# A graph network's convolutions on one core: one load of four places, addresses ahead of the last wait, fewer waits on wiped slices

## The chip, the cores and the metric

The kernel runs on 1 core of one Trainium2 chip. A core has TensorE (PE; its weight loads are listed as PEld), VectorE (DVE), ScalarE (ACT), GpSimd (POOL) and SyncE (SP), each with an instruction queue of its own, run by a sequencer. They meet only at semaphores. The metric is the device time of one execution in microseconds.

## The reference, cut to what matters

```python
# layer 0: layer norm, relu, an edge network, gather * message, segment sum, added to x
# layer 1: layer norm, relu, and then
def _rgcn_conv(x, src, dst, etype, basis, comp, root, bias):
    n = x.shape[0]                                    # 12500
    r = comp.shape[0]                                 # 8 relations
    W = jnp.einsum('rb,bio->rio', comp, basis)
    seg = dst * r + etype                             # 212500 edges
    agg = jax.ops.segment_sum(x[src], seg, num_segments=n * r)
    cnt = jax.ops.segment_sum(jnp.ones_like(seg, x.dtype), seg, num_segments=n * r)
    mean = (agg / jnp.maximum(cnt, 1.0)[:, None]).reshape(n, r, -1)
    return jnp.einsum('nri,rio->no', mean, W) + x @ root + bias
h = _rgcn_conv(x, src, dst, edge_type, basis1, comp1, root1, bias1)
h = jax.nn.relu(h)
out = _rgcn_conv(h, src, dst, edge_type, basis2, comp2, root2, bias2)
```

All features are 128 wide, all in float32. The two calls of `_rgcn_conv` are the two passes that the change touches; before them stand the sorting of the edges and layer 0.

## The kernel before, in words

`convolve` is called twice, with `which` = 0 and 1. The edges lie sorted by target. They are cut into 1661 columns of 128 edges (`NCOL`), four columns to a group (`TG`; the last group has one), 416 groups (`NG`). The 12500 nodes are 98 blocks of 128 (`NBLK`); a block's edges fill about 17 columns (`PERIOD`).

For each column, in every pass:

- GpSimd gathers the 128 source rows from DRAM into a slot of `got` (L2126). `got` holds 8 groups (`NGA`). GpSimd may gather group g when all columns up to group g - 8 have been through TensorE (`need(pool, s_pass, ...)`), so it runs up to 32 columns ahead.
- VectorE writes a one-hot matrix of the column's targets, `compare` (L2216), eight columns ahead, into `share` or `hot`.
- TensorE multiplies both into a PSUM bank of the column (L2138, two matmul instructions). In pass 0 it also counts the edges (L2141). Four banks are used in turn, so TensorE waits for the sum of the column four before (`s_sum`). It raises `s_pass`.
- VectorE adds the bank, 16 targets by 8 relations wide, to a ring of sums that holds six blocks (`RING`), at a place that was computed earlier and lies in SBUF: `add_column`. It reads the place into a register (`value_load`, L2231), forms the address (L2235, a register instruction), and adds (L2235, SCALAR_TENSOR_TENSOR). In pass 0 the counts are added with the sums, so this add is 128x256 instead of 128x128.

When a block's columns are complete (`closing_at(group)`), there is block work: TensorE spreads the inverse counts (L2165, two matmuls of 512 columns in each half), VectorE multiplies the block's slice of the ring by them (`weigh`, L2250, in two halves), ScalarE wipes the slice (L2191), TensorE multiplies by the eight relation matrices (L2157) and the root matrix (L2153), and SyncE stores the result and fetches rows of the next blocks.

What sets the order is each engine's program alone: it is written out by hand, unrolled, with no scheduler. `need` issues a wait if the value is above zero. Waits are gathered until the next instruction; where it has more of them than one instruction can carry, they become semaphore instructions of their own, recorded at L104.

An add must wait for three things beside its own bank: the preceding add (`s_sum`, since both can touch the same places), the wipe of the slice that the ring comes round to (`s_wiped`), and the join of the ring's 16 extra columns past its end to its beginning (`s_tail`, raised twice at each join).

## Time and profile before

| | us |
|---|---|
| median of 3 runs | 8354.52 (8352.68 to 8361.07) |
| span of the profiled execution | 8476.2 |
| TensorE busy (share) | 6081.7 (72%) |
| GpSimd busy | 5225.1 (62%) |
| VectorE busy | 4272.2 (50%) |
| ScalarE busy | 1968.7 (23%) |
| mean granted TensorE clock | 0.704 |

The profiled execution is one of its own, and the page gives its span, from first to last instruction; it is 121.7 us above the median of the timed runs. Shares are taken over the whole span, which has stages with different limits. The convolutions begin with the first gather of L2126. "Idle before" in a row is the time in which the engine did nothing just before these instructions, and the arrow names what ended it; "issue" there means that the profile shows nothing that the engine waited for. An engine's name with a q (DVEq) is its sequencer: such instructions aren't counted as busy.

### The profile page before, as it was taken

How to read it: one execution, taken by the hardware profiler on the slowest of the kernel's cores; microseconds unless marked ns; L12 is line 12 of the kernel's file. 1: busy time of each engine (PE TensorE's matmuls, PEld its weight loads, DVE VectorE, ACT ScalarE, POOL GpSimd, SP SyncE). 2: the span in 40 equal slices, each digit the busy share in tenths (PEclk: the TensorE clock that was granted, in tenths of full speed). 3: DMA queues.
4: the chain of work that ended last, by engine and by line, in shares of the span. 5: the costliest groups of instructions: out<-in, count | busy, mean ns of one | idle time of the engine just before them, and what ended most of it. 6: DMA issues, size and time to landing. Idle time of an engine off the chain costs nothing. (4 is left out here: it accounts for less than half of the span.)

```text
span 8476.2 us, 125307 instructions
## 1 busy us (share of the span) xinstructions
PE 6081.7 (72%) x31388; PEld 4489.2 (53%) x31388; DVE 4272.2 (50%) x13389; ACT 1968.7 (23%) x3891; POOL 5225.1 (62%) x5105
## 2 busy tenths in 40 slices
PE   5777777778888876777777877665666666666666
PEld 4555555556777765555555555443444444444444
DVE  6544454547888864554555555553333333333333
ACT  4444444445444433111111111110000000000000
POOL 3555555557888876666666666664665665665664
PEclk8877777779999987556556566666565565565666
DMA  5444444448999974111111111111111111111111
GB/s 148 128 131 124 130 125 126 118 111 180 190 192 191 188 162 146 50 51 49 50 50 50 50 49 51 50 50 37 48 48 47 48 49 47 47 48 47 47 48 38
DMA packets 816681, 750.03 MB, mean 88 GB/s; under 512 B 126421, under 2 KB 719249, under 8 KB 815637
## 3 DMA queue, kind: packets, MB, share of 16 engines
q1 hardware_dynamic: 578020, 401.11, 17.7%
q0 software_dynamic: 237296, 340.25, 17.6%
q8 instruction: 276, 4.52, 0.2%
q14 instruction: 459, 3.76, 0.1%
q10 hardware_dynamic: 630, 0.39, 0.0%
HBM read 574.58 MB, written 165.86 MB: 87 GB/s over the span
## 5 line engine op out<-in xcount | busy, mean ns | idle before, releaser
L2126 POOL DMA_INDIRECT got<-h_dram,etcol x3322 | 3147.7, 948 | 1993.1 <-issue 954.2
L2235 DVE SCALAR_TENSOR_TENSOR hacc<-bank,hacc 128x256 f32 (+1 forms) x3322 | 1185.0, 357 | 2839.8 <-issue 1463.1
L2138 PE MATMUL bank<-share,got 128*128 128x128 f32 x4436 | 1275.4, 410 | 773.4 <-DVE hacc L2235 535.9
L2138 PEld LDWEIGHTS bank<-share,got 128*128 128x128 f32 x4436 | 968.2, 278 | 1352.0 <-issue 1290.7
L1611 POOL DMA_INDIRECT msg_dram<-total,idx x1008 | 971.6, 964 | 869.9 <-DVE total L1362 596.6
L1626 POOL DMA_INDIRECT acc_dram<-total,idx x653 | 1023.5, 1567 | 214.3 <-issue 206.1
L2165 PE MATMUL bank<-rcnt,chosen 7*128 7x512 f32 (+45 forms) x784 | 738.5, 1040 | 461.8 <-DVE umade L2250 236.1
L2191 ACT ACTIVATE hacc<-ones_f 128x2048 f32<-128x2048 f32 (+1 forms) x196 | 290.8, 1483 | 2659.8 <-DVE umade L2250 1883.5
L2138 PE MATMUL bank<-hot,got 128*128 128x128 f32 x2208 | 633.8, 408 | 372.6 <-DVE hacc L2235 240.1
L2138 PEld LDWEIGHTS bank<-hot,got 128*128 128x128 f32 x2208 | 479.1, 275 | 657.0 <-issue 632.5
L2157 PE MATMUL bank<-wrel,umade 128*128 128x128 f32 x3136 | 684.2, 406 | 28.2 <-DVE umade L2250 25.0
L2157 PEld LDWEIGHTS bank<-wrel,umade 128*128 128x128 f32 x3136 | 633.5, 309 | 71.4 <-DVE umade L2250 46.8
L2216 DVE TENSOR_SCALAR share<-iota_f,dstcol 128x128 f32<-128x128 f32 x2218 | 659.2, 298 | 15.7 <-PEq L1970 10.6
L1358 DVE SCALAR_TENSOR_TENSOR soft<-bank,neg_b,log1p 128x512 f32<-128x512 f32 x416 | 311.5, 749 | 637.4 <-ACT log1p L1234 357.3
L1112 PEld LDWEIGHTS bank<-w,soft 128*128 128x128 f32 x3328 | 547.2, 233 | 74.4 <-issue 50.4
L1103 PE MATMUL bank<-edges_t,w 128*128 128x512 f32 x830 | 524.8, 714 | 50.8 <-issue 46.7
L1112 PE MATMUL bank<-w,soft 128*128 128x128 f32 x3328 | 542.7, 317 | 0.0
L2165 PEld LDWEIGHTS bank<-rcnt,chosen 7*128 7x128 f32 (+45 forms) x784 | 183.4, 290 | 559.0 <-issue 558.0
L1095 PE MATMUL bank<-ident,edges 128*128 128x128 f32 x1656 | 324.4, 307 | 154.1 <-issue 141.4
L2187 ACT ACTIVATE flat<-bank 128x128 f32<-128x128 f32 x196 | 54.4, 278 | 1610.7 <-issue 929.1
L1212 ACT ACTIVATE edges_t<-bank 128x512 f32<-128x512 f32 x414 | 248.0, 599 | 776.3 <-remote 682.6
L1128 PE MATMUL bank<-win,to_edge 128*128 128x128 bf16 x4992 | 396.9, 236 | 31.1 <-DVE total L1362 19.9
(263 smaller groups left out, 8275.8 us busy)
## 6 DMA issues: line engine op xcount, KB each, us to landing
edges<-in_edge_attr SPq DMA_DIRECT2D x415, 256.0 KB
unit<-msg_dram SPq DMA_DIRECT2D x616, 129.0 KB
got<-h_dram,etcol POOLq DMA_INDIRECT x3322
low<-rows_dram SPq DMA_DIRECT2D x164, 256.0 KB
win<-split_dram SPq DMA_DIRECT2D x416, 96.0 KB
low<-rows_dram SPq DMA_DIRECT2D x252, 128.0 KB
acc_dram<-zeros SPq DMA_DIRECT2D x200, 128.0 KB
made<-acc_dram SPq DMA_DIRECT2D x147, 128.0 KB, 3.2
```

What stands on the lines that cost most here:

```text
L1095: ins = nc.tensor.transpose(bank_t[:, j * P:(j + 1) * P], edges[s.slot(NE, 0)][:, j, :], g.ident[:, :])
L1103: nc.tensor.matmul(bank_z[s.slot(2, 1) if two_banks else 0][:, :], g.w1[:, :], edges_t[s.slot(2, 1)][:, :], start=True, stop=True).then_in ...
L1112: ins = nc.tensor.matmul(bank_e[:, j * F:(j + 1) * F], soft[k][:, j * P:(j + 1) * P], g.w2[:, :], start=False, stop=True, skip_group_check ...
L1128: ins = nc.tensor.matmul(bank[:, j * F:(j + 1) * F], to_edge[k][:, j, :], win[s.slot(NE, 2)][:, part * F:(part + 1) * F], start=windows.ow ...
L1611: pool.indirect_dma_start(g.msg_dram[:, :], bass.IndirectOffsetOnAxis(ap=idx[k][:, j:j + 1], axis=0), total[k][:, j, :], None).then_inc(s_ ...
L1626: pool.indirect_dma_start(g.acc_dram[j][:, :], bass.IndirectOffsetOnAxis(ap=idx[k][:, j:j + 1], axis=0), total[k][:, j, 0:F], None, comput ...
L2126: pool.indirect_dma_start(got[k][:, j, :], None, g.h_dram[which][:, :], bass.IndirectOffsetOnAxis(ap=source[:, c:c + 1], axis=0)).then_inc ...
L2138: ins = nc.tensor.matmul(columns[j][:, 0:P], got[k][:, j, :], equal, start=True, stop=True)
L2157: ins = nc.tensor.matmul(to, weighted[t % 2][:, r * P:(r + 1) * P], g.wrel[which][:, r * F:(r + 1) * F], start=False, stop=r == R - 1)
L2165: nc.tensor.matmul(bank_s, chosen[t % 2][0:t + 1, :], rates_all[0:t + 1, half * HALF:(half + 1) * HALF], start=True, stop=True).then_inc(s ...
L2216: v.tensor_scalar(hot[group % NHOT][:, j, :], g.iota_f[:, :], g.dstcol[:, c:c + 1], None, ALU.is_equal).then_inc(s_node, 1)
L2235: v.scalar_tensor_tensor(to, columns[j].rearrange("p (a n) -> p a n", n=NARROW), 1.0, to, ALU.mult, ALU.add).then_inc(s_sum, 1)
```

## The change

The places of a group are read by one load of four registers, without the assertion on their range. The address is formed ahead of the wait for TensorE's pass, which is now asked for last. The waits for the wiped slice and for the tail are issued only in groups where the number waited for has grown since the group before.

```diff
-            def add_column(c):
+            def load_places(group):
+                first = group * TG
+                _, at = nc.values_load_multi_w_load_instructions(
+                    place[:, first:first + g.columns(group)], engines=[mybir.EngineType.DVE], min_val=0, max_val=RING * P - 1,
+                    skip_runtime_bounds_check_because="a column's lowest target less the multiple of the ring's rows below it")
+                return at
+
+            def laps(group):
+                return len(range(RING, g.closed(group), RING))
+
+            def add_column(c, at):
                 group, j = divmod(c, TG)
-                if j == 0:
+                if j == 0 and (group == 0 or g.closed(group - 4) > g.closed(group - 5)):
                     need(dve, s_wiped, done_before + g.closed(group - 4))
-                    need(dve, s_tail, laps_before + 2 * len(range(RING, g.closed(group), RING)))
-                at = dve.value_load(place[:, c:c + 1], min_val=0, max_val=RING * P - 1)
+                if j == 0 and (group == 0 or laps(group) > laps(group - 1)):
+                    need(dve, s_tail, laps_before + 2 * laps(group))
                 to = ring[:, 0:SUMMED, bass.ds(at, NARROW)]
+                need(dve, s_sum, c)
+                dve.lower_ap(to)
                 dve.wait_ge(s_pass, c + 1)
-                need(dve, s_sum, c)
                 v.scalar_tensor_tensor(to, columns[j].rearrange("p (a n) -> p a n", n=NARROW), 1.0, to, ALU.mult, ALU.add).then_inc(s_sum, 1)
...
+                at = load_places(group) if group < NG else ()
                 for j in range(TG):
                     c = group * TG + j
                     if c < NCOL:
-                        add_column(c)
+                        add_column(c, at[j])
```

On VectorE, at the beginning of a group of the first pass in which a block is weighed, the order before is this. TENSOR_LOAD reads a place, "ISA x2" are a register instruction and the assert, "ISA" forms the address; `c_pass_0` and `c_sum_0` are `s_pass` and `s_sum`, `c_counts_0` is `s_wiped`, `u_left_0` is `s_tail`, `u_mm_0` and `c_low_0` are what TensorE raises in the block work.

```order
L2231 TENSOR_LOAD srccol [waits u_left_0,c_counts_0]
L2231 ISA x2
L2235 ISA [waits c_sum_0,c_pass_0]
L2235 SCALAR_TENSOR_TENSOR hacc<-bank,hacc 128x16x16
L2216 TENSOR_SCALAR hot_0<-iota_f,dstcol 128x128 [waits c_pass_0]
L2250 TENSOR_TENSOR umade_0<-bank,hacc 128x512 [waits u_left_0,u_mm_0,c_sum_0,c_low_0]
L2231 TENSOR_LOAD srccol
L2231 ISA x2
L2235 ISA [waits c_sum_0,c_pass_0]
L2235 SCALAR_TENSOR_TENSOR hacc<-bank,hacc 128x16x16
L2216 TENSOR_SCALAR hot_0<-iota_f,dstcol 128x128 [waits c_pass_0]
```

The same two columns of the same group after the change, on VectorE:

```order
L2229 TENSOR_LOAD srccol
L2246 ISA [waits c_sum_0]
L2248 SCALAR_TENSOR_TENSOR hacc<-bank,hacc 128x16x16 [waits c_pass_0]
L2216 TENSOR_SCALAR hot_0<-iota_f,dstcol 128x128 [waits c_pass_0]
L2263 TENSOR_TENSOR umade_0<-bank,hacc 128x512 [waits u_left_0,u_mm_0,c_sum_0,c_low_0]
L2246 ISA [waits c_sum_0]
L2248 SCALAR_TENSOR_TENSOR hacc<-bank,hacc 128x16x16 [waits c_pass_0]
L2216 TENSOR_SCALAR hot_0<-iota_f,dstcol 128x128 [waits c_pass_0]
```

The load stands once for the group, register instruction and assert are gone, and of the two waits on the address one has moved to the add. In this group neither the wiped slice nor the tail is waited for by the add. Over a pass, VectorE issues 415 loads, 1661 address instructions (96 with one more wait, 8 with two more) and the same adds, compares and block work. The other engines' programs are as before.

## Rows read from the trace of the kernel before

**Rows 1.** The page: the span, and GpSimd's gathers (busy, mean | idle before).

```profile
span 8476.2 us, 125307 instructions
L2126 POOL DMA_INDIRECT got<-h_dram,etcol x3322 | 3147.7, 948 | 1993.1 <-issue 954.2
```

**Rows 2.** Busy time by engine in two windows, first and second pass.

```profile
3289.00:5810.00 2521.00, 1863.06 (x7384) 1308.69 (x7384) 1260.96 (x3738) 265.93 (x388) 1574.46 (x1661) 0.61 0.19 49
5810.00:8457.00 2647.00, 1678.24 (x5774) 1178.81 (x5774) 981.66 (x3650) 161.64 (x296) 1573.26 (x1661) 0.60 0.18 47
```

**Rows 3.** Timeline of GpSimd (start, length): a run of 12 gathers, the next start.

```profile
5985.84 0.95 POOL L2126 DMA_INDIRECT got<-h_dram,etcol  x1 [1.63 <-PE bank L2138]
...
5999.59 0.95 POOL L2126 DMA_INDIRECT got<-h_dram,etcol  x1 [0.30 <-issue]
6004.59 0.95 POOL L2126 DMA_INDIRECT got<-h_dram,etcol  x1 [4.05 <-PE bank L2138]
```

**Rows 4.** Timeline of GpSimd: ends of the passes, and a short pause.

```profile
3289.03 1.04 POOL L2126 DMA_INDIRECT got<-h_dram,etcol  x1 [3.54 <-issue]
...
5774.23 0.95 POOL L2126 DMA_INDIRECT got<-h_dram,etcol  x1 [0.30 <-issue]
5835.05 0.98 POOL L2126 DMA_INDIRECT got<-h_dram,etcol  x1 [59.87 <-issue]
...
5888.91 0.94 POOL L2126 DMA_INDIRECT got<-h_dram,etcol  x1 [0.30 <-issue]
5891.35 0.94 POOL L2126 DMA_INDIRECT got<-h_dram,etcol  x1 [1.50 <-issue]
...
8425.34 0.95 POOL L2126 DMA_INDIRECT got<-h_dram,etcol  x1 [4.26 <-PE bank L2138]
```

**Rows 5.** The chain of waits (start, length, what), two adds in ordinary flow.

```profile
8409.53 0.29 DVE hacc L2235
...
8410.38 0.29 DVE hacc L2235
```

**Rows 6.** Busy time by engine (PE, PEld, DVE, ACT, POOL) around the run of rows 3.

```profile
5985.80:5992.20 6.40, 5.17 (x16) 2.85 (x17) 3.63 (x16) 0.28 (x1) 4.84 (x6) 0.72 0.23 62
5992.20:6002.80 10.60, 4.91 (x13) 2.58 (x12) 2.28 (x7) 0.00 (x0) 6.51 (x7) 0.50 0.19 50
6002.80:6010.60 7.80, 6.53 (x30) 5.92 (x30) 3.27 (x13) 1.35 (x2) 3.79 (x4) 0.60 0.13 34
```

**Rows 7.** The chain of waits late in a run of gathers.

```profile
8416.30 0.69 DVEq L2231
...
8419.84 0.70 DVEq L2235
```

**Rows 8.** Timeline of VectorE late in a run of 44 gathers, adds only.

```profile
5875.88 0.29 DVE L2235 SCALAR_TENSOR_TENSOR hacc<-bank,hacc 128x128 f32 x1 [6.51 <-issue]
...
5882.88 0.29 DVE L2235 SCALAR_TENSOR_TENSOR hacc<-bank,hacc 128x128 f32 x1 [6.51 <-issue]
...
5889.88 0.29 DVE L2235 SCALAR_TENSOR_TENSOR hacc<-bank,hacc 128x128 f32 x1 [6.51 <-issue]
...
5898.29 0.29 DVE L2235 SCALAR_TENSOR_TENSOR hacc<-bank,hacc 128x128 f32 x1 [7.92 <-issue]
```

**Rows 9.** Sequencer instructions, 5868 to 5890 us (ns min/median/max).

```profile
L2231 DVEq TENSOR_LOAD <-srccol x3: 690/707/707, 5873.0 to 5887.0; - x3
...
L2235 DVEq FUSED_REGOPS  x3: 701/710/710, 5871.6 to 5885.6; - x3
...
L104 DVEq EVENT_SEMAPHORE  x3: 702/702/702, 5870.2 to 5884.2; - x3
```

**Rows 10.** Sequencer instructions of line L2231 over the whole run.

```profile
L2231 DVEq TENSOR_LOAD <-srccol x3322: 1/301/1409, 3288.7 to 8455.9; - x196
...
L2231 DVEq SEQ_ASSERT  x3322: 1/23/1039, 3289.2 to 8456.5; - x196
```

**Rows 11.** All gathers, line L2126, by duration (ns min/median/max).

```profile
L2126 POOL DMA_INDIRECT got<-h_dram,etcol x3322: 942/947/1045, 3289.0 to 8425.3; - x196
```

## What I predict

> **What bounds the kernel now.** I read the page first, for where the time lies. The two convolutions run from 3289.0 us to the end at 8476.2, 5187 of 8476 us; no engine is busy over 75% of either [rows 1, 2]. They are what the change touches. GpSimd issues one gather per column, 3322 in all. Each call is busy 0.95 us and is followed by 0.30 us of its own; in an unbroken run the calls start 1.25 us apart [rows 3]. 1661 columns by 1.25 us are 2076 us. The first pass spends 2486 us from its first gather to the end of its last (3289.03 to 5775.2), the second 2591 us (5835.05 to 8426.3); between and behind stand tails of 59.9 and 49.9 us [rows 1, 4]. 2486 + 60 + 2591 + 50 = 5187. So GpSimd stands still for some 410 and 515 us, waiting for columns to be consumed (the ring `got` holds 8 groups of 4 columns). TensorE is busy 1863 and 1678 us [rows 2], by 98 blocks 19.0 and 17.1 us a block of 17 columns, where GpSimd needs 21.2 us. TensorE could keep up; VectorE's turn is what is late.
>
> Next the chain of waits, for VectorE's own pace. In ordinary flow one column takes 8410.38 - 8409.53 = 0.85 us [rows 5], and it is the sequencer's: load, register arithmetic, assert, semaphore, address (load and assert in [rows 10]), with the add of 0.29 us and the compare lying over them. 0.85 is under 1.25, so this pace alone doesn't hold GpSimd back. What does is seen in the second half of each long run of gathers. Take the run of [rows 6]: GpSimd starts a run of 12 calls at 5985.84 and ends it at 6000.54 [rows 3]. In its first 6.4 us VectorE starts 16 instructions; in the next 10.6 us only 7; then, with the run over, 13 in 7.8 us. The chain there shows why: each sequencer step of VectorE takes 0.70 us or a multiple of it, where an assert took 0.02 us and a load 0.30 [rows 7, 10]. In the long first run of the second pass (44 gathers without a pause) it settles at exactly 7.00 us a column [rows 8]. A column has five sequencer instructions there, each recorded at about 0.70 us [rows 9]. Where a group begins there is a sixth (a separate semaphore wait), and the distance is 8.41 us. So each sequencer instruction costs 1.40 us, two steps of 0.70, while the vector work itself costs nothing extra. It comes only while GpSimd has been issuing for a while, and ends about 2 us after it pauses. I call it stepping. It is what leaves VectorE behind, and it makes the number of *sequencer* instructions the quantity to count.
>
> **The change, part by part.** Counts are those of the emitted order.
>
> 1. One load for four places, no assert. Before, each column has a load, a register instruction and an assert; after, there is a load for each group: 3 x 1661 = 4983 become 415 a pass.
> 2. The address is computed ahead of the last wait. Before, two waits stand ahead of the add: one becomes a separate semaphore instruction, the other sits on the address. After, `s_sum` sits on the address and `s_pass` on the add itself, so 1661 separate instructions go. The handover from TensorE to the add no longer has the address computation in it; I give it no time, since GpSimd's pitch covers it.
> 3. Waits on a wiped slice and the tail only where the count has grown: of some 405 separate instructions a pass 104 remain (96 columns with one extra wait, 8 with two).
>
> The 192 products of a pass keep their two separate waits, 380 or so. Sequencer instructions a pass: 415 + 1661 + 104 + 380 = 2560, against 5 x 1661 + 405 + 380 = 9090. By column 1.54 against 5.47; in steps of 0.70 us 3.08 against 10.9. Vector work is the same. Nothing is moved on another engine.
>
> In ordinary flow the column falls from 0.85 us to about the two vector instructions (starts 0.2 to 0.35 us apart, with the wait for the preceding sum): I take 0.5 to 0.6. By itself that gains nothing, since GpSimd's 1.25 covers it; with stepping gone it would leave GpSimd as the bound. While stepping, a column falls from 7.6 us (10.9 x 0.70) to 3.08 x 0.70 = 2.16 us, which is still over 1.25.
>
> How much of the time is stepped? I treat it as a store that fills. Before: 6.4 us of ordinary flow are 7.5 columns, 82 steps, while 6.4 / 0.70 = 9 drain; so it holds about 72. After: TensorE allows (17 / 19.0 + 17 / 17.1) / 2 = 0.94 columns a us, so 2.90 steps a us come in and 1.43 drain; the store is full after 72 / 1.47 = 49 us instead of 6.4. In that time the consumers gain (0.94 - 0.80) x 49 = 6.9 columns on GpSimd. Then, stepping, the consumers take 1 / 2.16 = 0.46 a us, GpSimd catches up in 6.9 / 0.34 = 20 us and must pause. A stepped group takes 8.6 us and its gathers 5.0, so the pause is 3.6 us, and ends the state. A cycle of 49 + 20 + 4 = 73 us has 69.5 us of gathers: 1.25 x 73 / 69.5 = 1.317 us a column, 2188 us a pass. The tails empty the ring; at 0.6 instead of 0.85 us for up to 32 columns they lose 8 to 10 us each: 50 and 40.
>
> Sum: 3289 + 2 x 2188 + 90 = 7755 us, 721 below the profiled 8476.2. The timed median, 8354.5, lies 122 us below the profiled span already. I carry the difference over: 8354.5 - 721 = 7633 us.
>
> The load of four registers isn't in the trace. The nearest row is the load of one, 0.30 us [rows 10]. Its bounds are 0.30 and four times that, 1.2 us a group. Either lies under cover: a group needs 2 to 2.4 us of VectorE in ordinary flow and 5.0 of GpSimd. If while stepping it cost as four loads (eight steps), that would be 6 more steps a group, 4.58 a column. The same cycle is then 25 + 7 + 4 us, 1.39 us a column, 240 us more in all: 7875. I take two steps, as its row shows for one load.
>
> A rule that speaks against the change: a gather takes 942 to 1045 ns over both passes [rows 11], although VectorE runs one compare of 128x128 f32 for each. In the 6.4 us with 16 vector instructions its calls are as short as elsewhere [rows 3, 6]. So nothing is added to the sum. The Trainium skill, page "SBUF — State Buffer", section "Who interferes with whom", says that VectorE in a two-port mode takes a port pair from GpSimd for the whole instruction, and the section "SBUF: two separate sides" that GpSimd then can't write the descriptors of its DMAs. By that rule, compares that come closer together would lengthen the gathers, and the sum would be the 8339 us of the third rival. The trace doesn't agree with it here, by the rows just named.
>
> **The rivals.**
>
> *GpSimd alone (14%).* Stepping all but vanishes because small pauses empty the store each time. For: in the first pass, with runs of 8, TensorE's block work makes such pauses. Against: faster consumers leave no pause. 3289 + 2 x 2076 + 90 = 7531, less 122: 7409 us.
>
> *Stepping counts all instructions (16%).* 7.00 us are also seven instructions of 1.0 us. Against it stands the 8.41 us of the column with one wait more. After: 6210 instructions a pass, 3.74 a column. A store of 50 is full after 18.5 us, gained 3.5 columns are lost in 7 us, the pause is 4: 1.45 us a column, 2409 a pass. 3289 + 4818 + 90 - 122 = 8075 us.
>
> *No change (6%).* Either the gathers stretch: 0.28 us of each compare added, 1.53 us a column, 2541 a pass, 3289 + 5082 + 90 - 122 = 8339. Or stepping is the profiled run's own, and the timed runs hide the edit elsewhere. Against: without it the parts above would put the old kernel near 2076 a pass, 7.4 ms, and it measures 8.35.
>
> *Slower (4%).* Stepping never ends, since GpSimd's pauses become too short. It decides between 1.50 us, a pause (at 5890) after which the next column still took 8.41 us [rows 4, 8], and 4.05 us, after which it was back [rows 3, 6]. My 3.6 is near the latter. If it never ended, a column would take 2.16 us throughout, 3588 a pass: 3289 + 7176 + 90 - 122 = 10433 us.
>
> **How the numbers follow.** The described case has 60%: 7633 us; the rivals 14, 16, 6 and 4. The range reaches to the GpSimd floor below, and above past the dear load (7875) to near the all-instructions case: 7390 to 8010. Within 0.2% (17 us) counts as no change. Faster: 60 + 14 + 16 and a part of the 6, 0.92; same 0.04; slower 0.04.
>
> **What would show it.** In the new profile: about 6200 recorded instructions of VectorE's queue and engine a pass; a median gather still at 0.947 us; passes of some 2190 us; runs of gathers of 40 to 60 instead of 12; while stepping, a column of 1.75 us (2.8 at a group's first), against 3.7 if all instructions count. TensorE busy over 80%. I am wrong in mechanism if GpSimd's idle time stays above 250 us a pass, or if steps of 0.70 us come as often as before; in size if the runs end before 25 us.

## The result, and the profile after

The changed kernel takes 8117.9 us (median of 4 runs, 8113.1 to 8138.3), the kernel before 8353.6 (4 runs). The ratio is 0.9718, 95% interval 0.9698 to 0.9739: 236 us faster, where 721 were forecast. The time lies outside my range (7390 to 8010).

The page of the changed kernel gives the span, GpSimd's gathers and VectorE's adds (busy, mean | idle before):

```profile
span 8114.2 us, 112262 instructions
L2126 POOL DMA_INDIRECT got<-h_dram,etcol x3322 | 3147.5, 947 | 1726.8 <-issue 964.8
L2248 DVE SCALAR_TENSOR_TENSOR hacc<-bank,hacc 128x256 f32 (+1 forms) x3322 | 1181.4, 356 | 2762.2 <-remote 1460.2
```

The span has shrunk by 362 us, the timed value by 236. Part of the difference lies ahead of the change: the first gather starts at 3206.7 us, where the profile before had 3289.03 [rows 4]. The code there is the same; a profile of the old code with another product (bf1_before, below) has 3212.8. So some 80 of the 122 us by which the profile before stands above its timed runs lie ahead of the change and are of that one execution. The other 40 lie in its convolutions, so what the two profiles differ by there is some 40 us more than the timed runs gained. The convolutions went from 5187 to 4908 us. The ends of the passes, on GpSimd's timeline (start, length):

```profile
5634.26 0.95 POOL L2126 DMA_INDIRECT got<-h_dram,etcol  x1 [0.30 <-issue]
5688.20 1.00 POOL L2126 DMA_INDIRECT got<-h_dram,etcol  x1 [52.99 <-issue]
...
8076.49 0.95 POOL L2126 DMA_INDIRECT got<-h_dram,etcol  x1 [0.30 <-issue]
```

First pass 2428 us (before 2486), second 2389 (before 2591), tails 53.0 and 36.8 (before 59.9 and 49.9). That is 58 + 202 + 7 + 13 = 280 us; the other 82 of the 362 are those ahead of the first gather. GpSimd's work and its own pitch are as before [rows 1, 3]; what fell is its waiting, 1993 - 954 = 1039 to 1727 - 965 = 762 us, the tail between the passes included.

VectorE's sequencer no longer shows steps. Over the whole run (ns min/median/max), against [rows 9, 10]:

```profile
L2229 DVEq TENSOR_LOAD <-srccol x832: 320/343/481, 3206.4 to 8093.4; - x167
...
L2246 DVEq FUSED_REGOPS  x3322: 46/46/59, 3206.8 to 8093.8; - x196
```

The load of four registers costs 0.34 us, near my lower bound of 0.30. In the profile before, 1182 of VectorE's sequencer instructions last 0.66 to 0.74 us; here none does. Yet the adds still come in multiples of 0.70 us late in a long run of gathers. Timeline of VectorE in the run of 48 gathers with which the second pass begins, adds only:

```profile
5726.06 0.29 DVE L2248 SCALAR_TENSOR_TENSOR hacc<-bank,hacc 128x128 f32 x1 [5.10 <-remote]
...
5731.66 0.29 DVE L2248 SCALAR_TENSOR_TENSOR hacc<-bank,hacc 128x128 f32 x1 [5.12 <-remote]
...
5737.26 0.29 DVE L2248 SCALAR_TENSOR_TENSOR hacc<-bank,hacc 128x128 f32 x1 [5.11 <-remote]
```

5.60 us a column, eight steps, where [rows 8] had 7.00, ten. What ends the wait is now "remote", a releaser that the profile doesn't name; in the program it is `s_pass`, which TensorE raises. TensorE issues four instructions for the column there (an f32 product is two weight loads and two matmuls). Eight steps for four instructions is the price I had found for VectorE's.

In the ordinary cycle the same thing looks like a hold. TensorE, VectorE and GpSimd around the end of a run of 12 gathers that began at 6988.30:

```profile
6994.99 3.67 PE L2157 MATMUL bank<-wrel,umade 128*128 128x128 f32 x16
6998.50 1.06 PE L2138 MATMUL bank<-hot,got 128*128 128x128 f32 x8
7005.81 2.21 PE L2138 MATMUL bank<-share,got 128*128 128x128 f32 x8 [6.25 <-DVE hacc L2248]
```

```profile
7005.37 0.29 DVE L2248 SCALAR_TENSOR_TENSOR hacc<-bank,hacc 128x128 f32 x1 [10.38 <-remote]
```

```profile
7002.09 0.95 POOL L2126 DMA_INDIRECT got<-h_dram,etcol  x1 [0.30 <-issue]
7005.73 0.95 POOL L2126 DMA_INDIRECT got<-h_dram,etcol  x1 [2.70 <-remote]
```

The profile puts the four columns' products at 6998.50 to 6999.56, straight behind a block's 16 matmuls (and as many loads). The add that waits for the first of them starts at 7005.37, 5.8 us after the last is recorded as ended and 2.3 us after GpSimd's run has ended at 7003.04. The next columns take 0.42 to 0.60 us. This is no single case: in 103 pauses of GpSimd in this profile before which VectorE had added nothing for over 5 us, the next add comes a median of 2.3 us, at most 3.1, after the last gather has ended. I read it so: GpSimd fills what is free of its ring and stops, and the stop lets TensorE's results through. It is this pause that is left in the time. No experiment below removes this hold, so its cause is read from the rows, not shown.

### The profile page after: what moved, and what is told of

Same layout as the page of the kernel before. It is cut to its first block and busy times, and to the rows that moved or that the text cites. A ratio compares the mean times of both kernels' runs of the same rounds, so it can differ in the third digit from the quotient of the medians.

```text
span 8114.2 us, 112262 instructions
## 1 busy us (share of the span) xinstructions
PE 5797.3 (71%) x31388; PEld 4440.9 (55%) x31388; DVE 4125.7 (51%) x13389; ACT 1968.6 (24%) x3891; POOL 5224.3 (64%) x5105
## 5 line engine op out<-in xcount | busy, mean ns | idle before, releaser
L2126 POOL DMA_INDIRECT got<-h_dram,etcol x3322 | 3147.5, 947 | 1726.8 <-issue 964.8
L2138 PE MATMUL bank<-share,got 128*128 128x128 f32 x4436 | 1160.3, 399 | 716.6 <-DVE hacc L2248 437.1
L2138 PEld LDWEIGHTS bank<-share,got 128*128 128x128 f32 x4436 | 945.9, 277 | 1157.1 <-issue 1080.2
L1611 POOL DMA_INDIRECT msg_dram<-total,idx x1008 | 971.0, 963 | 784.6 <-DVE total L1362 513.9
L2165 PE MATMUL bank<-rcnt,chosen 7*128 7x512 f32 (+45 forms) x784 | 704.1, 995 | 399.3 <-issue 276.6
L2138 PE MATMUL bank<-hot,got 128*128 128x128 f32 x2208 | 583.8, 401 | 325.2 <-DVE hacc L2248 231.2
```

What stands on the lines that cost most here:

```text
L1611: pool.indirect_dma_start(g.msg_dram[:, :], bass.IndirectOffsetOnAxis(ap=idx[k][:, j:j + 1], axis=0), total[k][:, j, :], None).then_inc(s_ ...
L2126: pool.indirect_dma_start(got[k][:, j, :], None, g.h_dram[which][:, :], bass.IndirectOffsetOnAxis(ap=source[:, c:c + 1], axis=0)).then_inc ...
L2138: ins = nc.tensor.matmul(columns[j][:, 0:P], got[k][:, j, :], equal, start=True, stop=True)
L2165: nc.tensor.matmul(bank_s, chosen[t % 2][0:t + 1, :], rates_all[0:t + 1, half * HALF:(half + 1) * HALF], start=True, stop=True).then_inc(s ...
```

## The experiments

Eighteen kernels ran, on seven different chips, which differ in a way that I had not foreseen: on chips 2, 4, 11 and 14 the kernel before takes 8350 to 8529 us, as in the first measurement; on chips 12, 13 and 15 it takes 6957 to 6967, with the same code and the same data. I call the first the chips with steps.

### Half of the gathers, and a product in bf16: chip 13, without steps

I did not know that this chip has no steps when I wrote what follows. `half` leaves out every second gather (TensorE reads each even column twice), so the results are not the reference's:

```diff
-                for j in range(g.columns(group)):
+                for j in range(0, g.columns(group), 2):
...
-                pe.wait_ge(s_got[k], group // NGA * (16 * TG) + 16 * n + got_before[k])
+                pe.wait_ge(s_got[k], group // NGA * (8 * TG) + 16 * (-(-n // 2)) + half_before)
...
-nc.tensor.matmul(columns[j][:, 0:P], got[k][:, j, :], equal, ...)
+nc.tensor.matmul(columns[j][:, 0:P], got[k][:, j - j % 2, :], equal, ...)
```

`bf1` replaces the column's f32 product by one in bf16 (the upper halves of the same tiles), two TensorE instructions in place of four; `bf2` issues it twice, four again:

```diff
-                    ins = nc.tensor.matmul(columns[j][:, 0:P], got[k][:, j, :], equal, ...)
+                    ones16 = equal.bitcast(BF16).rearrange("p (n t) -> p n t", t=2)[:, :, 1]
+                    got16 = got[k][:, j, :].bitcast(BF16).rearrange("p (n t) -> p n t", t=2)[:, :, 1]
+                    for _ in range(1):          # bf2: range(2)
+                        ins = nc.tensor.matmul(columns[j][:, 0:P], got16, ones16, ...)
```

> The kernel before with a gather for every other column only (the same is left out). Theory 1: the ordinary flow alone, 0.85 us a column and TensorE's block work beside it, 20 to 21 us a block: 3206 + 98 x 41 + 100 = 7320 us, and slower than the changed kernel with half of the gathers by 300 us or more. Theory 2: 8300 to 8350 us.

> The changed kernel with a gather for every other column only; TensorE reads each gathered column twice (left out: half of the gathered rows, so the sums are of other rows). Theory 1 (runs of gathers longer than some 6 us hold back VectorE's sequencer and TensorE's completions in steps of 0.70 us; TensorE needs 8 steps a column in the second pass and 12 in the first): GpSimd is far ahead, in runs of 2, no column near 5.6 or 8.4 us, and the passes fall to TensorE's own 17 to 19 us a block: about 3206 + 98 x 36.5 + 100 = 6880 us. Theory 2 (the chain TensorE - VectorE - TensorE with its block work is itself the bound at 1.44 us a column, and GpSimd waits for it): 8050 to 8120 us.

> The changed kernel with the column's product in bfloat16, read from the upper halves of the float32 words: one weight load and one matmul a column instead of two and two (products are of truncated features). Theory 1: in the long first run 4 steps or 2.8 us a column in the second pass, 8 steps or 5.6 us in the first, and less waiting everywhere: 7550 to 7850 us. Theory 2 (TensorE's busy time): the column's 0.43 us become 0.11, 3300 x 0.32 us at most if all of it were on the path, so also faster; the pair with the next run tells them apart.

> The same bfloat16 product issued twice in a row into the same place (the second overwrites the first): two weight loads and two matmuls a column, as many instructions as float32 has, but half of its TensorE time. Theory 1: 5.6 us a column in the long first run of the second pass and 8.4 in the first pass, as in float32, and a time of 7950 to 8100 us, at least 150 us above the run with one. Theory 2: within 60 us of the run with one, since the difference is 0.11 us of TensorE a column under cover.

Measured: kernel before 6964.6 us; half_before 6567.5, ratio 0.9427 (0.9411 to 0.9443); half_after 5751.7, 0.8266 (0.8242 to 0.8290); bf1_after 6958.5, 0.9991 (0.9982 to 1.0001); bf2_after 6957.8, 0.9990 (0.9980 to 0.9999). Every absolute number that I expected failed, since the base had moved by 1390 us; that half_after would be over 300 us faster than half_before held (816 us). The bf1 and bf2 pair told nothing of steps, as there were none.

### The kernels as they are: chip 12, without steps

> The kernel before, unchanged, as a kernel of its own, for a trace beside the others. Theory 1 (the steps of 0.70 us are a condition of the chip or of the moment, not of the kernel): either 8350 us with passes of 2490 and 2590 us and steps of 0.70 us in the long gather runs, or some 6965 us with passes of 2076 to 2110 us, gathers 1.25 us apart nearly throughout, no steps, and a first gather at about 2750 us; nothing between. Theory 2 (a drift that grows and fades): a value between the two, with runs of gathers of 20 to 60 before a pause.

> The changed kernel, unchanged. Theory 1: 0.972 of the kernel before where that takes 8350 us; where it takes 6965, GpSimd's pitch of 1.25 us bounds both, VectorE's 0.85 or 0.42 us a column are both hidden, and only the tails and the first columns differ: 6955 to 6962 us, ratio 0.998 to 1.000. Theory 2: a ratio between 0.972 and 0.999.

> Of the change only the one load for four places without assert; the address is set after both waits and all waits on wiped slices and the tail stay. Where the steps come: VectorE has 2.25 queue instructions a column (semaphore wait, address, a quarter of a load), 4.5 steps, under TensorE's 8 and 12 steps, so the same as the whole change: 8100 to 8140 us (by the theory that only VectorE's queue counts: 8200 to 8260, the two other parts missing). Where they don't: 6955 to 6962 us, as all others.

> The changed kernel with one bf16 product a column in place of the f32 one, so TensorE has two instructions (load, product) where it had four. Where the steps come: 4 steps a column on TensorE, 2.8 us in place of 5.6 in a long gather run, 7550 to 7850 us if TensorE's steps are what is left of the wait, 8118 if its steps are not per instruction. Where they don't: 6958 us, as measured once.

Measured: kernel before 6966.6 us (33 runs); before_again 1.0002, after_again 1.0002 (both 0.9993 to 1.0011), load_only 0.9997 (0.9988 to 1.0006), bf1_again 0.9992 (0.9983 to 1.0001). Theory 1's second case: nothing between, and the change is worth nothing there (after_again and load_only lie 6 and 2 us above the 6955 to 6962 expected). The gathers in the page of before_again, then of after_again:

```profile
L2126 POOL DMA_INDIRECT got<-h_dram,etcol x3322 | 3147.6, 947 | 1053.6 <-issue 1007.9
```

```profile
L2126 POOL DMA_INDIRECT got<-h_dram,etcol x3322 | 3150.1, 948 | 1052.9 <-issue 1017.5
```

All but 35 to 46 us of the idle time is GpSimd's own 0.30 us behind each call. Its passes take 2080 and 2079 us before, 2080 and 2082 after, where I had worked out 2076 us as its floor. Windows of before_again over both passes (PE, PEld, DVE, ACT, POOL, clock, DMA) have TensorE busy for 80% and 74%:

```profile
2747.20:4865.50 2118.30, 1696.50 (x7433) 1244.32 (x7433) 1255.50 (x3747) 271.25 (x395) 1574.23 (x1662) 0.67 0.23 59
4865.50:6970.40 2104.90, 1560.50 (x5772) 1162.53 (x5772) 986.08 (x3646) 158.82 (x292) 1573.34 (x1661) 0.60 0.23 59
```

### Which part does it, when GpSimd is not the bound: chip 15, without steps

`half_load` and `half_addr` are half_before with one part of the change each.

> Half of the gathers left out as in half_before and half_after (TensorE reads each even column twice), so that GpSimd needs 1040 us a pass and the consumers bound it; of the change only the one load for four places without assert. Theory A (what a column costs there is the number of VectorE's queue instructions, most of them the load, the register and the assert instruction): most of the 816 us between the two half kernels, 5850 to 6000 us. Theory B (it is what stands between TensorE's last product and the add, that is the address behind the last wait): little of it, 6350 to 6500 us. On a chip with the steps of 0.70 us the kernel before shows 8350.

> The same half kernel with only the address set ahead of the last wait (each column still has its own load with assert, and all waits). Theory A: 6350 to 6500 us. Theory B: 5850 to 6000 us. If the two parts add up, this and the kernel with the one load together give 816 us less than 6567.

> The changed kernel with one bf16 product a column (two TensorE instructions for four), once more, in case this chip has the steps of 0.70 us: where the kernel before takes 8350 us, 7550 to 7850 if what is left of the wait is TensorE's steps by instruction, 8118 if not. Where the kernel before takes 6965 us: 6958 to 6962.

Measured: half_load 5965.1 us, 0.8571 (0.8557 to 0.8585); half_addr 6436.6, 0.9248 (0.9233 to 0.9264); bf1_third 0.9994 (0.9984 to 1.0004). The kernel before takes 6957.4 us on this chip, 6964.6 on chip 13, where the two other half kernels ran; I compare ratios. Against half_before's 0.9427 the whole change brings 0.1161 of the old time, the one load 0.0856 (74%), the address ahead of the wait 0.0179 (15%). The remaining 11% are the waits, which I did not try alone, or what the parts bring only together. Theory A holds: with the parts, VectorE's ordinary column (median distance of two adds, first and second pass) goes from 0.86 and 0.86 us to 0.79 and 0.79 with the address, 0.63 and 0.49 with the load, 0.56 and 0.43 with all, and the change is worth 816 us of 6567 as soon as GpSimd can deliver. The gathers of half_before, then of half_after, wait for columns to be consumed:

```profile
L2126 POOL DMA_INDIRECT got<-h_dram,etcol x1662 | 1573.2, 947 | 2211.4 <-PE bank L2142 1036.2
```

```profile
L2126 POOL DMA_INDIRECT got<-h_dram,etcol x1662 | 1573.5, 947 | 1405.3 <-PE bank L2142 829.6
```

Not all of the 816 us is time of VectorE's queue. Some 629 of them lie in the second pass, and there TensorE's granted clock rises too. The second pass of half_before, then of half_after:

```profile
4766.10:6529.40 1763.30, 1461.27 (x5623) 1076.92 (x5623) 943.89 (x3579) 153.23 (x284) 787.26 (x831) 0.67 0.15 39
4582.40:5717.20 1134.80, 1029.96 (x5641) 792.48 (x5642) 855.21 (x3584) 154.55 (x286) 786.15 (x831) 0.90 0.23 60
```

TensorE is busy for 83% of the pass before and 91% after, at a clock of 0.67 and 0.90, and the same work keeps it busy 431 us less. How much the shorter queue would bring at an unchanged clock was not measured.

### The TensorE side, on chips with steps: 14 and 11

> The kernel before with one bf16 product a column in place of the f32 one: two TensorE instructions fewer a column, VectorE's queue as before. Where the steps of 0.70 us come (kernel before at 8350): in the second pass VectorE's 10 steps a column stand above TensorE's (8, now 4), so nothing is won there; in the first pass TensorE's 12 steps become 8, and VectorE's 10 to 12 take over: 8250 to 8354 us. If TensorE's instructions were not counted there: 8354. Where the steps don't come (6965): GpSimd's 1.25 us a column is the bound, 6955 to 6966 us.

> The changed kernel with one bf16 product a column, where the change leaves VectorE three queue instructions a column and the product TensorE two. If this chip has the steps of 0.70 us (kernel before near 8360): theory 1 (after the change TensorE's own instructions, stepped, are the wait that is left) 7550 to 7850 us, 2.8 us a column in a long gather run in the second pass where the changed kernel showed 5.6; theory 2 (the changed kernel's wait is a fixed delay of the handover, whatever is issued) 8118 and 5.6 us. If it has none (kernel before near 6965): 6958.

Measured: on chip 14 bf1_before 8399.2 us, 1.0042 of the kernel before (1.0023 to 1.0062), against 8250 to 8354 expected; it is slower, by 39 us. On chip 11 bf1_fourth 8242.9 (two runs), 0.9666 (0.9638 to 0.9694), against 7550 to 7850. Both totals were missed, but the columns are where the count of instructions puts them: bf1_fourth's stand at 2.80 us late in the long first run of the second pass and at 5.60 in the first. For bf1_before the *first* pass decides. The kernel before has three columns of 8.40 us in a row there:

```profile
3321.59 0.43 DVE L2235 SCALAR_TENSOR_TENSOR hacc<-bank,hacc 128x256 f32 x1 [7.67 <-issue]
3329.99 0.43 DVE L2235 SCALAR_TENSOR_TENSOR hacc<-bank,hacc 128x256 f32 x1 [7.78 <-remote]
3338.39 0.43 DVE L2235 SCALAR_TENSOR_TENSOR hacc<-bank,hacc 128x256 f32 x1 [7.79 <-remote]
```

and bf1_before has this:

```profile
3255.59 0.42 DVE L2237 SCALAR_TENSOR_TENSOR hacc<-bank,hacc 128x256 f32 x1 [6.38 <-remote]
3262.59 0.42 DVE L2237 SCALAR_TENSOR_TENSOR hacc<-bank,hacc 128x256 f32 x1 [6.23 <-issue]
3269.59 0.42 DVE L2237 SCALAR_TENSOR_TENSOR hacc<-bank,hacc 128x256 f32 x1 [6.38 <-issue]
```

7.00 us: TensorE's 12 steps have become 8, and VectorE's 10 are now the longer.

### Does a denser or looser row of gathers matter: chip 14

`paced1` is the changed kernel with a small memset behind each gather:

```diff
+        idle = sb("idle", [P, 1 * TG * NG], mybir.dt.uint8)
...
+                    for at in range(c * 1, c * 1 + 1):
+                        nc.gpsimd.memset(idle[:, at:at + 1], 0)
```

> The changed kernel with one small memset (128x1, 0.10 us by the page) on GpSimd behind each gather, so that the gathers start some 1.36 us apart in place of 1.25. If this chip has the steps (kernel before at 8350 or more): theory 1 (they come from gathers that follow each other without a gap) they vanish, a pass takes 1.36 x 1661 = 2259 us, 0.935 to 0.945 of the kernel before; theory 2 (only a pause of 3 us in which GpSimd works at nothing ends them, a memset is no pause) the hold on TensorE's instructions comes as before and each column costs 0.1 us more, 0.995 to 1.015 of the kernel before. If it has none (6965): GpSimd's pitch is the bound, 6965 + 2 x 1661 x 0.11 = 7330 us, 1.052.

Measured: 8274.9 us (two runs) where the kernel before takes 8510.0, 0.9725 (0.9697 to 0.9753), in neither theory's range. The changed kernel itself was not run beside it. The experiment did not do what it should. GpSimd's timeline in an ordinary run of gathers shows why:

```profile
6500.98 0.12 POOL L2130 MEMSET idle<- 128x1 uint8 x1
6501.29 0.95 POOL L2127 DMA_INDIRECT got<-h_dram,etcol  x1 [0.19 <-issue]
6502.54 0.94 POOL L2127 DMA_INDIRECT got<-h_dram,etcol  x1 [0.19 <-issue]
```

The memset fits into the 0.30 us between two gathers, and the pitch stays 1.25. So theory 1 isn't tested. But late in the long first run of the second pass the picture is another. GpSimd's gathers, then VectorE's adds:

```profile
5891.31 0.94 POOL L2127 DMA_INDIRECT got<-h_dram,etcol  x1 [0.19 <-issue]
5893.36 0.94 POOL L2127 DMA_INDIRECT got<-h_dram,etcol  x1 [0.99 <-issue]
5894.76 0.94 POOL L2127 DMA_INDIRECT got<-h_dram,etcol  x1 [0.34 <-issue]
5896.89 0.94 POOL L2127 DMA_INDIRECT got<-h_dram,etcol  x1 [1.06 <-issue]
```

```profile
5896.70 0.29 DVE L2251 SCALAR_TENSOR_TENSOR hacc<-bank,hacc 128x128 f32 x1 [2.35 <-remote]
5899.57 0.29 DVE L2251 SCALAR_TENSOR_TENSOR hacc<-bank,hacc 128x128 f32 x1 [2.38 <-remote]
5902.40 0.29 DVE L2251 SCALAR_TENSOR_TENSOR hacc<-bank,hacc 128x128 f32 x1 [2.34 <-remote]
```

GpSimd's own gathers now start up to 2.1 us apart, though they wait for nothing that the profile shows, and a column falls to 2.84 us, half of the changed kernel's 5.60. In the first pass, with six TensorE instructions a column, it falls to 3.56 in place of 8.40. Before that, both had reached the old level or come near it (5.60 and 7.72). So two steps for each instruction are not a fixed price: with one more instruction of GpSimd's between two gathers it came down to about one. The time shows nothing of this, and what the memset costs or gains as a whole can't be told without the changed kernel on the same chip.

### The parts of the change on a chip with steps: 4

> Of the change only the one load for four places without assert; address behind both waits, all waits on wiped slices and the tail. If the chip has the steps (kernel before at 8350 or more): VectorE's queue has 2 instructions a column and a load a group, 4 to 4.5 steps, under TensorE's 8 (second pass) and 12 (first pass). Theory 1 (the slower of the two queues, counted in steps, sets the column; after the change that is TensorE) nearly the whole gain, 0.972 to 0.978 of the kernel before, and 5.60 us a column late in the long first run of the second pass. Theory 2 (each queue instruction that VectorE loses gains its share: 2.75 of the 3.93 that the whole change takes away) 0.980. If it has none: 1.000.

> Of the change only the address set ahead of the last wait; each column keeps its load, register instruction and assert, and all waits stay. If the chip has the steps: VectorE has four queue instructions a column (load, register, assert, address), 8 steps, as many as TensorE in the second pass and fewer than its 12 in the first. Theory 1: 5.60 us a column late in the long first run of the second pass, where the kernel before shows 7.00, so most of the gain in the stepped columns, but an ordinary column stays near 0.8 us, so less reaches the ring between two holds: 0.982 to 0.990. Theory 2: 1 of 3.93 instructions: 0.993. If it has none: 1.000.

The edits are the load with its callers alone, and these lines alone:

```diff
+                need(dve, s_sum, c)
+                dve.lower_ap(to)
                 dve.wait_ge(s_pass, c + 1)
-                need(dve, s_sum, c)
```

Measured: kernel before 8355.8 us; load_steps 0.9746 (0.9729 to 0.9763), addr_steps 0.9828 (0.9812 to 0.9845). Theory 1's ranges hold for both; theory 2's 0.993 for the address alone is far off, its 0.980 for the load is outside the interval. The decisive rows are addr_steps' adds late in the long run of the second pass:

```profile
5750.74 0.29 DVE L2236 SCALAR_TENSOR_TENSOR hacc<-bank,hacc 128x128 f32 x1 [5.06 <-remote]
...
5756.34 0.29 DVE L2236 SCALAR_TENSOR_TENSOR hacc<-bank,hacc 128x128 f32 x1 [5.12 <-remote]
...
5761.94 0.29 DVE L2236 SCALAR_TENSOR_TENSOR hacc<-bank,hacc 128x128 f32 x1 [5.01 <-remote]
```

One queue instruction less and the column falls from 7.00 to 5.60; take away 1.75 or 2.75 more (load_steps, the whole change) and it stays at 5.60. That is a maximum of two queues, not a sum. The times agree: the load alone has 0.0254 of the gain and the address alone 0.0172, together more than the 0.0266 to 0.0282 of the whole change (on other chips with steps).

### Both on one chip: 2, with steps

> The changed kernel with one bf16 product a column, on the same chip as the changed kernel itself. If the chip has the steps: theory 1 (two TensorE instructions fewer a column count as long as they are stepped, but the hold that follows a block's 32 instructions of L2159 does not depend on them) 0.4 to 0.8% under the changed kernel, 0.964 to 0.968 of the kernel before; theory 2 (0.9666 and 0.9718 differed by the chip) within 0.2% of it. If it has none: 0.999, within 0.2% of it.

> The changed kernel, unchanged, beside the one with the bf16 product. If the chip has the steps: 0.970 to 0.974 of the kernel before, as measured first, also if the kernel before takes 8510 and not 8355 us here. If it has none: 1.000.

Measured: kernel before 8349.5 us; after_last 8124.1, 0.9734 (0.9721 to 0.9747); bf1_last 8101.6, 0.9702 (0.9689 to 0.9716). The bf16 product is 22 us, 0.3%, under the changed kernel; the runs don't overlap (8094.5 to 8104.7 against 8119.5 to 8132.7). That is more than theory 2 and less than theory 1 expected. It is the fastest version with all gathers on the chips with steps, but it gives the gathered values in bf16, which the changed kernel does not. Adds of bf1_last in the long run of the second pass:

```profile
5705.00 0.29 DVE L2250 SCALAR_TENSOR_TENSOR hacc<-bank,hacc 128x128 f32 x1 [2.31 <-remote]
5707.80 0.29 DVE L2250 SCALAR_TENSOR_TENSOR hacc<-bank,hacc 128x128 f32 x1 [2.31 <-remote]
5710.60 0.29 DVE L2250 SCALAR_TENSOR_TENSOR hacc<-bank,hacc 128x128 f32 x1 [2.31 <-remote]
```

2.80 us, half of 5.60, for half the instructions. The stepped column of all kernels, late in the first long run of each pass (queue instructions of VectorE / weight loads and matmuls of TensorE, two steps of 0.70 us each):

| kernel | first pass: counts, longer x 1.40 | measured | second pass: counts, longer x 1.40 | measured |
|---|---|---|---|---|
| before | 5 / 6, 8.40 | 8.40 | 5 / 4, 7.00 | 7.00 |
| bf1_before | 5 / 4, 7.00 | 7.00 | 5 / 2, 7.00 | 7.00 |
| addr_steps | 4 / 6, 8.40 | 8.39 to 8.41 | 4 / 4, 5.60 | 5.60 |
| load_steps | 2.25 / 6, 8.40 | 7.68 to 8.40 | 2.25 / 4, 5.60 | 5.60 |
| changed | 1.25 / 6, 8.40 | 8.40 | 1.25 / 4, 5.60 | 5.60 |
| bf1_last | 1.25 / 4, 5.60 | 5.60 | 1.25 / 2, 2.80 | 2.80 |
| paced1 | 1.25 / 6, 8.40 | 3.53 to 3.56 | 1.25 / 4, 5.60 | 2.83 to 2.87 |

The measured columns are a handful in each pass, those where the distance has settled. paced1 doesn't fit the rule. TensorE's separate semaphore instruction, one a column, isn't among its counts; with it bf1_last would have 3 and the changed kernel 5.

Why halving the column's steps brings so little is seen in the cycle of bf1_last. TensorE's block work and its columns:

```profile
6865.69 0.26 PE L2141 MATMUL bank<-share,got 128*128 128x128 bf16 x1 [9.48 <-DVE hacc L2250]
...
6874.96 3.78 PE L2159 MATMUL bank<-wrel,umade 128*128 128x128 f32 x16
6878.53 0.63 PE L2141 MATMUL bank<-share,got 128*128 128x128 bf16 x4
6888.69 0.27 PE L2141 MATMUL bank<-share,got 128*128 128x128 bf16 x1 [9.52 <-DVE hacc L2250]
```

Once a block (here every 23.0 us) the 16 f32 products of L2159 and the four columns behind them are held: TensorE stands for 9.5 us, and the next add comes at 6888.25, 3.0 us after GpSimd's run has ended at 6885.27. With half of the column's instructions this hold is no shorter than the changed kernel's shown above (VectorE stood for 10.4 us there, for 12.4 here). What a block's 32 instructions have in it was not tried by taking them away. TensorE's granted clock falls besides, as its busy time does. The two windows of after_last, then of bf1_last:

```profile
3207.00:5690.00 2483.00, 1749.56 (x7433) 1297.74 (x7433) 1182.24 (x3742) 270.01 (x393) 1570.84 (x1661) 0.63 0.20 50
5690.00:8090.00 2400.00, 1519.24 (x5678) 1130.00 (x5678) 899.33 (x3615) 155.42 (x288) 1569.14 (x1661) 0.62 0.20 51
```

```profile
3207.00:5690.00 2483.00, 1362.49 (x5784) 839.94 (x5784) 1198.59 (x3772) 271.19 (x395) 1584.32 (x1675) 0.55 0.20 50
5690.00:8090.00 2400.00, 1158.87 (x4092) 710.78 (x4093) 872.78 (x3621) 158.81 (x292) 1557.01 (x1647) 0.55 0.20 51
```

The mean granted clock is 0.55 of full speed in place of 0.63 and 0.62, so TensorE stood most of the time at the lower of its two levels, 1.2 GHz, with 1362 and 1159 us busy in place of 1750 and 1519, and the mean f32 matmul of the block's product takes 427 ns in place of 404. That this is also why bf1_before is 0.4% slower than the kernel before fits (its clock is 0.55 and 0.54), but was not tested by itself.

## Why the prediction was wrong, point by point

- *What bounds the kernel.* Right for the profile that I had: GpSimd stands still for consumers, and VectorE's queue steps by 0.70 us. "TensorE could keep up; VectorE's turn is what is late" is the step that failed. I took TensorE at its unstepped 17 to 19 us a block, and so at 0.94 columns a us in the cycle. But TensorE's instructions step as VectorE's do, two steps each. The rows were there: [rows 2] have 5774 matmuls and 5774 weight loads in the second pass, 118 for each of its 98 blocks. At 1.40 us each they would need 165 us a block, where GpSimd needs 21. No pace of VectorE's makes that good. I could also have seen the 8.40 us of the first pass, three columns in a row, which are more than VectorE's ten steps; a sixth VectorE instruction, my reason for the one 8.41 us of [rows 8], stands only where a group begins. bf1_before shows that they were TensorE's six.
- *The stepped column.* Forecast 1.75 us (2.8 at a group's first), 2.16 with the block work. Measured 5.60 in the second pass and 8.40 in the first, by TensorE's 8 and 12 steps. VectorE's own part is now hidden; where it still showed, in bf1_before and before, its count of five held. That a step count is no fixed price, paced1 shows.
- *The store of 72 steps, full after 49 us.* It failed with it: it was worked out from VectorE's instructions alone. (By its own terms, 1.25 x 73 / 69.5, it gives 1.313 us a column and not 1.317, 7 us less a pass.) The runs of gathers are mostly 8 to 16 long, not 40 to 60, and the pitch over a pass is 2428 / 1661 = 1.46 and 2389 / 1661 = 1.44 us, not 1.317. Against 2188 that is 240 and 201 us, the term that was mis-sized: 441 of the 485 us by which 7633 falls short of 8118. The tails are off by 3 each, in opposite directions. The rest is the offset: I carried 122 us over in full, which puts the first gather at 3289 - 122 = 3167 where it is at 3206.7 (40 us), and the timed median stands 4 above the profiled span.
- *Ordinary flow.* Forecast 0.5 to 0.6 us, measured 0.56 to 0.64 in the first pass and 0.42 to 0.43 in the second. Right in size, but I had called it worth nothing by itself. On chip 4, load_steps and addr_steps have the same settled columns (5.60 us in the second pass), and load_steps, whose ordinary column is 0.49 to 0.64 us against 0.74 to 0.80, is faster by 65 us. The likely reason is that more columns get through between two holds. How the 236 us divide between stepped columns and ordinary flow is not shown: the parts overlap, and the columns at the full 7.00 us are few. What the profiles say is where the gain lies, 58 us in the first pass, where the settled column is 8.40 us before and after, and 202 in the second.
- *The load of four registers.* 0.34 us, unstepped: the dear case didn't come.
- *Tails.* Forecast 50 and 40, measured 53.0 and 36.8.
- *The rule on the shared port.* As forecast, nothing of it: with compares 0.42 us apart in ordinary flow the gathers' mean is 947 ns, 948 before. No run here shows the interference that the Trainium skill, page "SBUF — State Buffer", section "Who interferes with whom", describes.
- *The rivals.* "Stepping counts all instructions" gives 8075, the nearest number, for a wrong reason: its stepped column would be 3.7 us. On the chips without steps GpSimd is the bound before the change as well as after, so that nothing is gained: what "GpSimd alone" says of the bound and "no change" of the ratio is so there, but neither for its own reason nor with its number. Against the second I had argued that without steps the old kernel would have to measure some 7.4 ms; on three chips it measures 6.97. "Slower" did not come: pauses such as the one of 2.70 us shown above, which are shorter than my 3.6, were enough.
- *The sign I had named for being wrong in mechanism* was GpSimd's idle time above 250 us a pass; it is 352 and 313 (2428 and 2389 less 2076). TensorE busy over 80% did not come either: 1765 us of the first pass with its tail and 1535 of the second are 71% and 63%. The 6200 recorded instructions of VectorE a pass came (some 6320 and 6220), with 416 loads a pass where I had counted 415.

Open are three things. What makes the steps is not settled, nor whether they belong to the chip or to the moment: no chip was seen in both conditions, but chip 14 gave 8360 and later 8510 us for the same kernel. One rival stands untested: the times of the experiments each have a recorded span 1.7 us below them, so they seem to come from executions that the profiler recorded, and a cost of writing the records themselves would also go by the number of instructions. No time is known to be without it. And a wider spacing of all gathers was not reached: paced1 widened them only late in its long runs.

## What to carry to other kernels

When instructions of one engine are seen to take a multiple of their usual time, count the instructions of every engine that works in the same stretch before pricing a cut, and take the longest: what was hidden beneath the first is the next bound. Work out too what the kernel would take without the trouble; an edit that is worth 2.8% here is worth nothing where GpSimd's 1.25 us a gather is the bound, and 12% where half of the gathers are gone (with a faster TensorE clock as part of it). Look late in the long runs of an experiment too, not only at its total: paced1's time looked like the changed kernel's, while its stepped columns took half as long. And measure on more than one chip before an absolute time is forecast.

## What the runs showed of the hardware

- The same kernel takes 8350 to 8529 us on four chips and 6957 to 6967 on three. In the profile before, VectorE's queue has 1182 instructions of 0.66 to 0.74 us, in before_again 2; each of the 1182 starts within 6.7 us after the start of an indirect DMA of GpSimd's. The difference is not in the convolutions alone: the first gather starts at 3206.7 us in the changed kernel's profile and at 2747 in before_again's, and the scatters of L1611 are preceded by 785 and 327 us of idle time. Whether steps make that difference too was not looked into. From the page of the changed kernel, then of before_again:

```profile
L1611 POOL DMA_INDIRECT msg_dram<-total,idx x1008 | 971.0, 963 | 784.6 <-DVE total L1362 513.9
```

```profile
L1611 POOL DMA_INDIRECT msg_dram<-total,idx x1008 | 977.2, 969 | 327.1 <-issue 272.4
```

- On a chip without steps both passes of 1661 gathers with hardly a pause leave VectorE and TensorE at full pace, so a long row of gathers alone is not the cause.
- Late in a long run of gathers a queue instruction of the longer queue takes 1.40 us with gathers alone and about 0.70 with a memset behind each, when the gathers themselves start up to 2.1 us apart (paced1).
- The adds that wait for TensorE's results come late while its instructions are recorded at their usual pace: products at 6998.5, the add that waits for them at 7005.4, 2.3 us after the gathers paused. In such a stretch a matmul's recorded end says nothing of when its semaphore comes.
- A memset of 0.12 us fits into the 0.30 us behind an indirect DMA: in ordinary runs the pitch stays 1.25 us.
